# Attention maxima turned by VectorE in 32-wide blocks, values of one key tile at a time, shared products in every second step

## What is computed

```python
xn = layernorm(x)
# attention: 16 heads of 16; every projection has rank 32
def holo(x, basis, phase, amp): return (x @ basis.T) @ (amp * cos(phase)).T
q, k, v = holo(xn, ...q), holo(xn, ...k), holo(xn, ...v)      # split into heads
attn = softmax(q @ k.T * 0.25)                                # (8, 16, 512, 512)
attention = holo(attn @ v, ...o)
# feed-forward: 8 experts of 352, best 2 of each token, and a shared MLP of 704
ffn = sum over the 2 best of weight * (silu(xn @ wg) * (xn @ wu)) @ wd
shared = (silu(xn @ sw_gate) * (xn @ sw_up)) @ sw_down
out = x + attention + ffn + shared
```

## Time and profile before

| | us |
|---|---|
| median of three runs | 946.4 (944.36 to 946.92) |
| the profiled execution | 944.99 |
| its span, first to last instruction | 943.2 |
| TensorE matmul busy | 871.3 (92%) |
| VectorE busy | 608.0 (64%) |
| ScalarE busy | 583.3 (62%) |
| GpSimd busy | 427.3 (45%) |
| mean granted TensorE clock | 0.969 of full |

### The profile page before, as it was taken

The page is one execution under the profiler, slowest core; times in us unless marked ns, Lnnn a source line. Parts: engine busy times, 40 slices in busy tenths (PEclk is TensorE's granted clock), DMA queues, the critical chain, the costliest instruction groups (busy, mean ns, idle before and its releaser), DMA issues.

```text
span 943.2 us, 19555 instructions
## 1 busy us (share of the span) xinstructions
PE 871.3 (92%) x6491; PEld 605.1 (64%) x6492; DVE 608.0 (64%) x914; ACT 583.3 (62%) x941; POOL 427.3 (45%) x417
## 2 busy tenths in 40 slices
PE   5846999999999989889999999999999999999996
PEld 2436999999999976456556555555565465565462
DVE  6787844444444455676786786786777877776752
ACT  5855744444444442767767767767767866856764
POOL 2104722222222151753753764854754844744831
PEclk9965999999999999999999999999999999999997
DMA  9884555222222216554854755755755655654310
GB/s 315 315 265 149 187 151 172 72 72 68 76 67 69 65 47 171 157 154 101 203 158 118 198 159 127 198 155 130 189 163 130 192 161 130 191 141 109 76 48 23
DMA packets 91479, 133.74 MB, mean 142 GB/s; under 512 B 17512, under 2 KB 51824, under 8 KB 91024
## 3 DMA queue, kind: packets, MB, share of 16 engines
q1 hardware_dynamic: 84720, 114.95, 43.3%
q0 software_dynamic: 6480, 17.70, 7.1%
q10 hardware_dynamic: 208, 0.14, 0.0%
HBM read 76.10 MB, written 51.56 MB: 135 GB/s over the span
## 4 chain that ended last, share of the span: by engine, by line
PE 80%; DVE 11%; issue 3%; ACT 2%; DMA 2%; POOL 1%; DVEq 0%; ACTq 0%; POOLq 0%
PE bank L1463 12%; PE bank L1503 10%; PE s_pair L1412 9%; PE bank L1359 8%; PE s_pair L1341 8%; PE bank L1568 7%; PE st_pair L1491 6%; PE st_pair L1341 6%; DVE top L1934 4%; PE bank L1349 2%; PE bank L1324 2%; DMA xg<-xn_rows,token_of 1%; PE bank L1476 1%; PE bank L1517 1%; PE bank L1402 1%
## 5 line engine op out<-in xcount | busy, mean ns | idle before, releaser
L1934 DVE TENSOR_REDUCE top<-s_pair 128x2 f32<-128x1024 f32 x248 | 303.7, 1225 | 134.1 <-PE s_pair L1412 131.2
L1120 ACT ACTIVATE prob<-st_pair 128x1024 f32<-128x1024 f32 x252 | 259.1, 1028 | 116.9 <-PE st_pair L1491 109.1
L780 POOL DMA_INDIRECT xg<-xn_rows,token_of x71 | 82.7, 1165 | 207.5 <-PE bank L1324 157.3
L1463 PE MATMUL bank<-xT_b,w_sh 64*128 64x512 f32 x960 | 143.2, 404 | 0.5
L1412 PE MATMUL s_pair<-k_rows,q_rows 48*128 48x512 f32 x496 | 115.6, 459 | 12.0 <-DVE top L1934 11.8
L1503 PE MATMUL bank<-prob,v_ones 128*32 128x512 f32 x1024 | 124.8, 605 | 0.0
L1463 PEld LDWEIGHTS bank<-xT_b,w_sh 64*128 64x128 f32 x960 | 91.7, 187 | 31.1 <-issue 8.3
L1491 PE MATMUL st_pair<-q_rows,k_rows 50*128 50x512 f32 x504 | 106.2, 415 | 3.4 <-ACT prob L1120 2.6
L1359 PE MATMUL bank<-w_exp,c_hT 128*128 (+1 forms) x639 | 94.2, 292 | 0.6 <-ACT c_y L1027 0.6
L1412 PEld LDWEIGHTS s_pair<-k_rows,q_rows 48*128 48x128 f32 x496 | 47.4, 184 | 64.9 <-DVE top L1934 55.4
L1341 PE MATMUL s_pair<-w_exp,xg_T 128*128 x468 | 88.1, 338 | 0.0
(11 more groups left out here) (238 smaller groups left out, 1240.6 us busy)
## 6 DMA issues: line engine op xcount, KB each, us to landing
qk_rows<-qk_hi SPq DMA_DIRECT2D x56, 256.0 KB
q_rows<-qk_rows SPq DMA_DIRECT2D x64, 192.0 KB
k_rows<-qk_rows SPq DMA_DIRECT2D x56, 192.0 KB
expert_rows<-c_y SPq DMA_DIRECT2D x71, 128.0 KB, 1.7
qk_rows<-qk_lo SPq DMA_DIRECT2D x28, 256.0 KB
x_all<-in_L_attn_x_dram SPq DMA_DIRECT2D x8, 512.0 KB, 7.3
xn_rows<-x_n SPq DMA_DIRECT2D x8, 512.0 KB, 3.5
o_b<-in_L_attn_x_dram SPq DMA_DIRECT2D x8, 512.0 KB, 6.5
```

The lines of the kernel that those rows point to most:

```text
L780: pool.indirect_dma_start(xg[s % 4][:, :], None, xn_dram, bass.IndirectOffsetOnAxis(token_of[:, s:s + 1], 0)).then_inc(c_x[s % 4], 16)
L1120: act.activation(prob[n % 3][:, 2 * jp:2 * jp + 2, :].rearrange("p j l -> p (j l)"), score_T_pair(b, g, t)[:, :], ACT.Exp, scale=HD ** -0. ...
L1463: ins = pe.matmul((g_bank, u_bank)[up][:, :], w_sh[rows, a, o:o + P], xT_of(b)[rows, c, k, :], start=(n == 0 and i == 0), stop=(n == 1 and ...
L1934: dve.tensor_reduce(top[g % 2][:, :, jp, qt], score_pair(b, g, v)[:, :].rearrange("p (i k) -> p i k", i=2), AX_X, ALU.max).then_inc(d_max, 1)
```

## The change

- `split_max` no longer ends with the parts: after the subtract VectorE waits for it and for the DMA that last read this `top_T`, and then makes four transposes of [32, 32] into `top_T` (now plain float32). `turn_max` on TensorE and `max_rows` on ScalarE are gone, and the semaphores b_mt and a_mt with them; `load_max` waits for the new d_mt. Waits of the users of `m_bank` name the reader that is now the last.
- `values` takes one key tile at t = 2, 4, 6 (tiles 0, 1, 2) and tile 3 at t = 0 of the next slot; each counts on b_pv.
- `CUTS` is (0, 6, 12): piece 0 at t%4 = 1, piece 1 with the swap ahead of it at t%4 = 3, nothing of a pair at even t.
- `DOWN_CUTS` is (0, 12, 17, 29, 34): 12 at t%4 = 1, 5 at 2 (behind values and the small matmuls), 12 at 3 with the one swap ahead, 5 at 4. The order is plain: the whole first half, then the whole second.

```diff
             def load_max(b, g):
-                wait(sp, a_mt, b * NG + g + 1)
+                wait(sp, d_mt, b * NG + g + 1)
...
-            def max_rows(b, g):
-                wait(act, b_mt, b * NG + g + 1)
...
-            def turn_max(b, g):
-                wait(pe, d_m, b * NG + g + 1)
...
-                pe.transpose(m_bank[0:32, 0:P], top_parts[g % 2][:, :, :, :, :].rearrange("p i a j t -> p (i a j t)").bitcast(F32),
-                             ident_f[:, :]).then_inc(b_mt, 1)
-
-            CUTS = (0, 5, 6, 7, 12)
-            DOWN_CUTS = (0, 10, 15, 20, 32, 34)
+            CUTS = (0, 6, 12)
...
-                if kt % 2:
-                    ins.then_inc(b_pv, 1)
+                ins.then_inc(b_pv, 1)
...
-            FROM_LAST = len(DOWNS) - 2
-            DOWN_ORDER = [(0, i) for i in range(FROM_LAST)] + [(1, i) for i in range(len(DOWNS))] + [(0, i) for i in range(FROM_LAST, len(DOWNS))]
-            assert (DOWN_CUTS[2], DOWN_CUTS[4]) == (FROM_LAST, FROM_LAST + len(DOWNS))
+            DOWN_ORDER = [(n, i) for n in range(2) for i in range(len(DOWNS))]
+            DOWN_CUTS = (0, 12, 17, 29, 34)
...
-                if piece in (2, 4):
-                    pe.wait_ge(b_ha, swaps(b, SFT + 2 * pair) + piece // 2)
+                if piece == 2:
+                    pe.wait_ge(b_ha, swaps(b, SFT + pair) + 1)
...
-            def piece(b, g, t, n):
+            def piece(b, g, t):
                 what, c, j = unit(b, g, t // 4) if t % 4 else unit_before(b, g, t // 4)
...
+                if what == "down":
+                    down_pair(c, j, (t - 1) % 4)
+                elif what == "pair" and t % 2:
+                    gate_up_shared(c, j, t % 4 // 2)
+                elif what == "odd" and t % 4 == 1:
+                    gate_up_both(c)
+                elif what == "odd" and t % 4 == 3 and there(c - 1):
+                    low_rank_o(c - 1)
...
                     if t % 4 == 0:
                         next_score(b, g, t)
-                        piece(b, g, t, 4)
+                        piece(b, g, t)
                     if t == 0 and there(pb):
-                        values(pb, pg, 2)
                         values(pb, pg, 3)
-                    if t == 4 and now:
-                        values(b, g, 0)
-                        values(b, g, 1)
-                    if t == 4 and there(nb):
-                        turn_max(nb, ng)
+                    elif t % 2 == 0 and t:
+                        values(b, g, t // 2 - 1)
                     if (g, t) == (1, 0) and now:
                         project_values(b, 1)
-                    if t % 4 == 1:
-                        piece(b, g, t, 0)
                     if t % 4 == 2:
-                        piece(b, g, t, 1)
                         small(b, g, t)
-                        piece(b, g, t, 2)
-                    if t % 4 == 3:
-                        piece(b, g, t, 3)
+                    if t % 4:
+                        piece(b, g, t)
...
             def split_max(b, g):
                 wait(dve, d_max, b * 32 + g * 8 + 8)
-                wait(dve, b_mt, b * NG + g - 1)
+                wait(dve, d_mt, b * NG + g - 1)
...
+                wait(dve, d_m, b * NG + g + 1)
+                wait(dve, m_in[g % 2], (2 * b + g // 2) * 32)
+                for r in range(0, P, 32):
+                    ins = dve.transpose(top_T[g % 2][:, r:r + 32], dst[r:r + 32, :, :, :, :].rearrange("p i a j t -> p (i a j t)").bitcast(F32))
+                ins.then_inc(d_mt, 1)
```

More of the change, by code:

```diff
@@ L261, in build_program @@
         top_parts = [sb(f"top_parts{i}", [P, 2, 2, 2, TPB], F32R, late) for i in range(2)]
-        top_T = [sb(f"top_T{i}", [32, P], F32R, late) for i in range(2)]
+        top_T = [sb(f"top_T{i}", [32, P], F32, late) for i in range(2)]
         xT_bs = [xT_b, xT_1]
@@ L1104, in values_out @@
                 wait(act, b_v, b * 2 + half + 1)
-                wait(act, b_pv, (b - 1) * 8 + (half + 1) * 4)
+                wait(act, b_pv, (b - 1) * 16 + (half + 1) * 8)
                 act.activation(v_ones[:, :, half * 8:half * 8 + 8, 0:HD],
@@ L1524, in project_values @@
                     wait(pe, r_in, b * 48 + 48)
-                    wait(pe, a_mt, b * NG + 1)
-                    if b == 0:
-                        pe.wait_ge(d_r, 2)
+                    wait(pe, d_r, b + 2) if there(b + 1) else wait(pe, d_po, (b - 1) * 2)
                 elif there(b + 1):
@@ L1561, in down_pair @@
                     f = q
[L1562 removed]
+                    if n == 0 and pair == 0 and (i == 0 or q != DOWNS[i - 1][0]):
                         wait(pe, p_h, lows(b, q)) if q != BOTH else wait(pe, d_hl, b + 1)
@@ L1628, in next_score @@
                     score(qb, qg, t - STEPS + AHEAD)
-            def piece(b, g, t, n):
+            def piece(b, g, t):
                 what, c, j = unit(b, g, t // 4) if t % 4 else unit_before(b, g, t // 4)
-                if t % 4 == 0:
-                    if what == "down":
-                        down_pair(c, j, 4)
-                elif what == "pair":
-                    gate_up_shared(c, j, n)
-                elif what == "down":
-                    down_pair(c, j, n)
-                elif what == "odd":
-                    if n == 0 and there(c):
-                        gate_up_both(c)
-                    if n == 3 and there(c - 1):
-                        low_rank_o(c - 1)
+                if what == "down":
[6 more added lines that the diff above has]
+                    low_rank_o(c - 1)
             def small(b, g, t):
@@ L1698, in _ @@
             pe.wait_ge(c_hed, NS)
-            for n in range(3):
-                gate_up_shared(0, 0, n)
+            gate_up_shared(0, 0, 0)
             score(0, 1, 1)
-            gate_up_shared(0, 0, 3)
+            gate_up_shared(0, 0, 1)
             score(0, 1, 2)
@@ L1705, in _ @@
             score(0, 1, 3)
-            for n in range(4):
+            for n in range(2):
                 gate_up_shared(0, 1, n)
```

58 lines of the change are left out of this document (21 added, 37 removed).

## The result

The changed kernel takes 980.2 us (median of four runs, 977.96 to 982.12), the kernel before in the same session 946.7 (944.36 to 948.04): ratio 1.0357, 95% interval 1.0329 to 1.0385, 33.5 us slower. In a later session the same two gave 980.3 and 944.2, ratio 1.0336 (1.0272 to 1.0400). The forecast was 952, slower by 6, range 935 to 967. The direction was right, the size more than five times too small.

What follows compares the result with a forecast made beforehand. Neither VectorE nor TensorE alone was taken to bind; it changes by step. +0.7 a batch gives +5.2, GpSimd +3, start and end -2.1: +6 on 944.99 is 951, as a median 952; range 935 to 967.

Steps and rivals of the forecast that it cites:

- the mechanism of step 4: Attention slot, t = 4: VectorE's chain replaces TensorE's, so 2.4 us falls only to 2.26 to 2.3, -0.75 a batch.
- Step 0: First of a slot's eight steps, score pair to score pair: loses a block of values, 2.2 to 1.74 us in g = 0.
- steps 2 and 6: Attention steps t = 2 and 6: each gains a block of values, 1.99 us against 1.82; sum +2.1 a batch.
- steps 3 and 7: Attention steps t = 3 and 7, with products and two score pairs: keep about 2.2 us, priced at 2.18.
- Odd steps with pairs: Attention steps with six product pairs instead of five: 1.95 us against 1.82, +0.13 five times a batch.
- The rival in which lone blocks are free of their entrance: Attention steps 1, 2, 5 and 6 mostly stay at 1.82: -12 us, with the ends 933; chance 0.24.
- The swaps: In down, 16 swaps fewer: taken as 0, bounds 0 to -0.1 each, at most -2 us in all.
- The forecast's queue: VectorE's work behind the split in step 3: four transposes 0.1 apart move it by 0.5 us, bounds 0.4 to 0.95.
- the third rival: VectorE's transposes follow like dependent instructions, 0.95 instead of 0.5 a slot: +14, 966; chance 0.18 together with GpSimd's lock.
- GpSimd's lock: VectorE's cast and subtract wait for GpSimd, with no slack left in step 4: +3 us, bounds 0 to +8.
- the clock: Rival: idle of 0.9 us in step 4 halves TensorE's clock; if each slot paid, +54 us, 1006; chance 0.05.
- start and end: First turn leaves TensorE's path, -0.6; one block of values moves before the last exponents, -1.5; together -2.1 us.

Runs made afterwards that it cites:

- The turn alone: The kernel before with only the turn of the maxima moved to VectorE, values, products and swaps as before: 960.8 us, ratio 1.0179.
- the run with one block: The changed kernel with one transpose instead of four, three quarters of the maxima left out: 949.2 us, ratio 1.0048 against the kernel before.
- the run with extra work: The changed kernel with the score pair of step 4 computed four times over: 972.4 us, against 980.3 for the unaltered changed kernel beside it.
- The order alone: The kernel before with the new order of values and products and one swap, TensorE still turning the maxima: 945.1 us, ratio 0.9996.
- values alone: The kernel before with values one key tile at a time, old cuts and both swaps, TensorE turning the maxima: 972.8 us, ratio 1.0290.

## Why the prediction was right and wrong

*Right: the mechanism of step 4.* VectorE's chain takes the place of TensorE's, and nearly the whole gain of the values is lost. The turn alone gives the same 2.77 with both blocks of values in the step.

*Right: the prices of TensorE.* Step 0 went to 1.74 in g = 0 and 1.94 in g = 1 (forecast 1.74 and 1.92), steps 2 and 6 to 1.98 to 2.09 (1.99), the step with project_o to 2.7 (2.69), the low-rank product to 3.15 (3.12), project_values(0) to 2.15 (2.15), steps 3 and 7 to 2.15 to 2.26 (2.18). Odd steps with pairs came to 1.96 to 2.09 (1.95). The rival in which lone blocks are free of their entrance, 933 us, did not come true: each change of tile shape costs its tenth here too. The swaps were worth 0, as taken.

*Wrong: the transposes are not independent small instructions.* The step that failed is "I take 0.1 apart", from the four of the earlier trace rows and from qk_low, which starts 0.09 into the subtract in the earlier trace rows. The groups of the changed kernel, 450 to 880 us:

```profile
L1905 DVE STREAM_TRANSPOSE top_T<-top_parts 32x32 f32<-32x32 f32 x92 | 18.4, 200 | 1.7
```

Each takes 0.200 us (0.199 to 0.203 over all 128), each starts 0.212 to 0.216 after the one before it, and qk_low, or what stands in its place, starts 0.03 after the end of the last. The forecast's queue moved by 0.5; it moved by 1.0, 0.05 above the upper bound of 0.95. So, where GpSimd holds nothing, step 4 is 2.78 instead of 2.3: 0.47 x 4 = 1.9 us a batch. This was the third rival, priced at +14.
The section The DRAIN you can't avoid of the Trainium skill's "VectorE: DVE Perf Modes" has each instruction wait for an empty pipe, and adds that a next one that is not held starts earlier. For the transposes the trace agrees with the first (13 ns from one's end to the next one's start), for what follows the subtract or the lone transpose with the second (0.09 into 0.18; 0.14 into 0.20, 585.79 to 585.93). I had let the rows of other instructions speak for the transposes.

The starts behind the transposes narrow the cause. The four read rows 0, 32, 64 and 96 upward of `top_parts`. After the fourth, qk_low and its like (whose inputs start at row 0) begin 0.03 after its end, in 27 slots; in the other five the maximum follows, which reads only PSUM, and it begins 0.06 before that end. After the lone transpose of the run with one block, which reads rows 0 to 31, qk_low and its like begin 0.06 before its end, in 27 slots too. An instruction waited here where its input in SBUF starts at other rows than the last one's. That it is this, and not the kind of instruction, is a reading of these starts; no run changed it by itself.

*Partly wrong: GpSimd's lock.* Charged at +3 in all, bounds 0 to +8. In g = 0 step 4 is 3.2 to 4.4 us instead of 2.78, since a subtract or a cast is held there. By the medians that is 0.55 us a batch; summed over the traced execution, with one step of g = 1, it is 7.6 us, of which the kernel before had 1.4. So the charge was some 3 us too small, within its bounds. The casts and subtracts themselves are held little longer than before (7.5 us beyond their undisturbed lengths in all, for 6.0); what is new is that nothing covers it. What the chapter of the Trainium skill "SBUF — State Buffer" calls the shared port pair does not take in the transposes, which kept their 0.200 us in the 21 that lie wholly within an arithmetic instruction of GpSimd.

*Wrong: the clock.* It was a rival of its own with 0.05, "if each slot paid". Not each slot paid but about one in four: one stretch a batch, five of six times in g = 0, where the wait is longest. In steps 5 and 6 there it makes 2.90 and 2.69 (medians) out of 2.09 and 1.99: 1.5 us a batch. The rival treated the idle as the forecast had it, 0.9 us a slot; with transposes of twice the length it is 1.4, and with the lock on top 1.8 to 3.0. The failure was to price the rivals as alternatives when one makes the next likelier: slow transposes lengthen the wait, the lock lengthens it further, and behind the longest waits the clock was halved.

*The sum, by the table's medians.* Forecast +0.7 a batch and 0.4 for the lock; measured +5.3 (69.7 to 75.0). The gap of 4.2 is 1.9 of transposes, 1.5 of clock, 0.15 of lock (0.55 for 0.4) and 0.3 of odd steps (2.09 instead of 1.95, twice); 0.35 is spread over steps too small to name. One by one the first seven sequences grew by 4.9 to 6.9 us, 39.6 in all, more than seven times 5.3 since the medians leave out the longest holds. The profiled span grew by 37.1, so start and end give 2.5 back (forecast 2.1).

*Signs named beforehand.* The weight loads' wait grew as said, ScalarE's turn went, the transposes did not come 0.1 apart, and the granted clock left 1.00 between 380 and 920 us, which was named as a sign of being wrong.

*What stays open.* With the turn alone step 4 of g = 0 is as long (3.21) and the clock stays, which is read as the idle within it, since two blocks of values fill it there; the run with extra work supports that. It is not the whole rule. The order alone, with step 4 at 1.83, has two such stretches too, at 477.4 and 549.1, each after a single step of 2.9 us or more; the changed kernel keeps its clock behind the step 4 of 4.30 us of its first g = 0; the turn alone keeps it behind an idle of 2.0 us; and the run with extra work keeps it through a stretch in which TensorE was busy 1.17 of 3.40. The stretches of 3.4 or 6.8 us between 410 and 417, which most of the traces show and that of the kernel before does not, were not looked into. How much idle, and of what shape, was not settled.

## What to carry to other kernels

Price a kind of instruction that the trace does not hold at its whole duration, one after the other, until a trace of that kind shows it overlapping; another kind's overlap is no evidence, nor, by the starts seen here, that of instructions that all read from the same first row. Before work is taken from the engine that covers a slow chain elsewhere, ask how long that engine will then stand still, at its worst place and not on average, since on TensorE the idle may cost twice: once as a wait and once as clock. Price rivals that feed one another as one case too, and widen the range to it. The prediction did price slow transposes rightly, at +14; what it left out was what they would set off.

## What the runs showed of the hardware

- A transpose of 32 x 32 float32 by VectorE takes 0.200 us; four from different rows follow one another every 0.213 us. With their way in and out four of them put 1.0 us into VectorE's chain; the one transpose by matmul that they replace cost 0.22 on TensorE.
- VectorE's transposes are not held by GpSimd (0.199 to 0.203 us throughout), while casts and subtracts of 16 elements are, one cast through several GpSimd instructions in a row, for 4.53 us.
- A matmul pair of another tile shape than its neighbours costs 0.34 to 0.43 us, one among its like 0.23 (values alone).
- More work did not make the kernel slower and probably made it faster: with 0.7 us of repeated matmuls in each step 4 five of six stretches at half clock were gone from the trace, and the median was 972 instead of 980 us, with intervals that overlap.
